# The gate of a Mamba block taken from VectorE: a copy on ScalarE and a product on GpSimd in its place

## What is computed

```
xi = silu(conv(xi) + conv_b)                 # 96 channels, L = 1024 steps
dbl = xi @ xp_w.T ;  dt, Bm, Cm = split(dbl)
delta = softplus(dt @ dt_w.T + dt_b)
dA = exp(delta * A) ; dBu = delta * Bm * xi
h  = dA_t * h + dBu_t                        # scan over L, 16 states a channel
y  = sum_s(h * C) + xi * Dp
y  = y * silu(z)                             # the gate
out = y @ out_w.T
```

## Time and profile before

| | |
|---|---|
| median of 3 runs | 4874.72 us |
| lowest and highest | 4870.76 and 4888.22 us |
| the profiled execution | 4889.31 us, of it 4886.7 us span on the core |
| granted TensorE clock, mean | 0.892 of full speed |
| busy PE, DVE, ACT, POOL | 85%, 74%, 57%, 48% |

### The profile page before, as it was taken

One profiled execution on the slowest core, in us unless ns is written; L12 is line 12 of the kernel. 1 busy time (PEld: TensorE's weight loads), 2 busy tenths in 40 slices (PEclk: granted clock), 3 DMA queues, 4 the chain that ended last, 5 costly groups with the idle time before them and its releaser, 6 DMA issues.

```text
span 4886.7 us, 48989 instructions
## 1 busy us (share of the span) xinstructions
PE 4157.1 (85%) x14248; PEld 1532.0 (31%) x14248; DVE 3639.2 (74%) x3157; ACT 2766.8 (57%) x3396; POOL 2334.7 (48%) x1084
## 2 busy tenths in 40 slices
PE   6779986899869998599986999769986799867997
PEld 2422233222332223322233222332233322332223
DVE  1469966699657996499864998559976599666996
ACT  2556645566455666466564664656646566465554
POOL 0137642467315773066630776227752376424663
PEclk9889998899878999799896998979998899987888
DMA  1147641567316772177622775237851476405661
GB/s 38 40 115 184 161 102 38 142 165 176 85 35 165 170 173 63 51 172 173 150 54 71 174 171 143 70 77 167 185 131 41 109 176 167 110 12 136 147 161 48
DMA packets 166840, 580.30 MB, mean 119 GB/s; under 512 B 22460, under 2 KB 23208, under 8 KB 162952
## 3 DMA queue, kind: packets, MB, share of 16 engines
q1 hardware_dynamic: 152168, 538.66, 46.0%
q10 hardware_dynamic: 14336, 37.76, 2.6%
HBM read 467.12 MB, written 71.48 MB: 110 GB/s over the span
## 4 chain that ended last, share of the span: by engine, by line
issue 30%; POOL 29%; PE 22%; ACT 9%; DVE 8%; DMA 1%; POOLq 0%; SPq 0%; DVEq 0%; ACTq 0%
POOL arena L1380 26%; PE ps L499 3%; PE ps L554 3%; PE ps L595 2%; PE ps L649 2%; DVE arena L1291 2%; ACT arena L819 2%; PE ps L545 2%; PE ps L714 2%; ACT arena L837 1%; POOL arena L1370 1%; PE ps L573 1%; PE ps L529 1%; POOL x L1388 1%; PE ps L695 1%
## 5 line engine op out<-in xcount | busy, mean ns | idle before, releaser
L1380 POOL TENSOR_TENSOR arena<-arena 128x1024 f32<-128x1024 f32 x768 | 1860.7, 2423 | 984.0 <-DVE arena L1291 984.0
L1291 DVE TENSOR_TENSOR_SCAN arena<-arena,ps 128x1024 f32<-128x1024 f32 x768 | 1756.3, 2287 | 96.1 <-ACT arena L994 1.0
L994 ACT ACTIVATE arena<-arena,a_all 128x1024 f32<-128x1024 f32 x768 | 867.2, 1141 | 427.0 <-DVE arena L1291 280.9
L1286 DVE TENSOR_TENSOR ps<-ps,arena 128x1024 f32<-128x1024 f32 x768 | 931.0, 1212 | 177.0 <-PE ps L697 176.2
L695 PE MATMUL ps<-arena,spread 32*128 32x512 f32 x1536 | 904.9, 677 | 130.6 <-DVE arena L1291 80.2
L697 PE MATMUL ps<-arena,spread 32*128 32x512 f32 x1536 | 891.5, 678 | 0.0
L714 PE MATMUL ps<-arena,gather 128*32 128x512 f32 x3072 | 550.1, 661 | 39.6 <-POOL arena L1380 39.6
L760 PE MATMUL ps<-x 96*96 96x512 f32 x1008 | 506.4, 621 | 0.0
L695 PEld LDWEIGHTS ps<-arena,spread 32*128 32x128 f32 x1536 | 235.7, 192 | 780.0 <-issue 386.8
L649 PE MATMUL ps<-arena,w_in 96*96 96x512 f32 x512 | 325.7, 795 | 65.6 <-DMA arena<-xq 64.8
L1334 POOL TENSOR_TENSOR x<-x,arena 96x512 f32<-96x512 f32 x64 | 109.4, 1709 | 431.9 <-DVE arena L1130 431.9
(11 more groups left out here) (158 smaller groups left out, 5672.2 us busy)
## 6 DMA issues: line engine op xcount, KB each, us to landing
arena<-dl SPq DMA_DIRECT2D x768, 512.0 KB, 5.8
dl<-arena ACTq DMA_DIRECT2D x64, 384.0 KB, 6.3
x<-pn SPq DMA_DIRECT2D x56, 247.5 KB, 6.0
arena<-in_x SPq DMA_DIRECT2D x9, 1536.0 KB, 10.6
arena<-xq SPq DMA_DIRECT2D x64, 192.0 KB, 7.9
arena<-arena ACTq DMA_DIRECT2D x64, 192.0 KB, 5.5
out<-x SPq DMA_DIRECT2D x64, 192.0 KB, 2.1
arena<-xq SPq DMA_DIRECT2D x64, 191.8 KB, 6.7
```

The costliest lines, as they stand in the source:

```text
L994: act.activation(da[:, m % DAS, :], dbc[:, m % DBC, :], ACT.Exp, scale=a_all[:, v // 2, m:m + 1]).then_inc(da_ready, 1)
L1286: dve.tensor_tensor(driven, driven, bmat[:, v % 2, :], ALU.mult).then_inc(bu_ready, 1)
L1291: dve.tensor_tensor_scan(hs[:, m % HSS, :], da[:, m % DAS, :], driven, 0.0, ALU.mult, ALU.add).then_inc(h_ready, 1)
L1380: pool.tensor_tensor(product, product, cmat[:, v % 2, :], ALU.mult).then_inc(pr_ready, 1)
```

## The change

The product y * silu(z) is split. ACT copies y from banks 0 and 1 to `yz` (`copy_y`, in slot `ACT_Y` = 2, ahead of that slot's decay; new semaphore `y_copied`), with the two waits that the gate had. POOL multiplies `yz` by `sz` in place (`gate`, in slot `POOL_GATE` = 1 behind that slot's product and ahead of `mix`), and `yz_ready` is now POOL's. PE's `skip` waits for `y_copied`. ACT's silu(z) leaves slot 1 and becomes the first work of slot 3 (`silu_z`, called by `early`), with a load of the silu table ahead and one of the exp and ln table behind it; the pair's first unit keeps it where it was. At the end of the pair the copy on ACT stands ahead of `mix_bias`, and the product on POOL ahead of `mix`.

```diff
-S_GATE, S_SKIP = 2, 3
+ACT_Y, POOL_GATE, S_SKIP, ACT_SILU_Z = 2, 1, 3, 3
...
                     if v:
-                        pe.wait_ge(yz_ready, p * UNITS + v)
+                        pe.wait_ge(y_copied, p * UNITS + v)
...
+                def silu_z(v):
+
+                    V = p * UNITS + v
+                    if v >= 2:
+                        act.wait_ge(yz_ready, V - 1)
+                    for c in range(2):
+                        act.wait_ge(z_ps, 2 * V + c + 1)
+                        act.activation(part(sz[:, v % 2, :], c), ps[0:DI, 6 + c, :],
+                                       ACT.Silu).then_inc(sz_ready, 1)
+
                 def early(slot, v):
...
+                    if slot == ACT_SILU_Z and v:
+                        act.preload_act_table(ACT.Silu)
+                        silu_z(v)
+                        exp_table()
...
-                        if v >= 2:
-                            act.wait_ge(yz_ready, V - 1)
-                        for c in range(2):
-                            act.wait_ge(z_ps, 2 * V + c + 1)
-                            act.activation(part(sz[:, i, :], c), ps[0:DI, 6 + c, :],
-                                           ACT.Silu).then_inc(sz_ready, 1)
+                        if v == 0:
+                            silu_z(v)
                         exp_table()
...
+                def copy_y(v):
+
+                    V = p * UNITS + v
+                    act.wait_ge(y_acc, (V + 1) * GPB)
+                    if v >= 2:
+                        act.wait_ge(mo_ready, 2 * (p * QUADS + v // 2))
+                    act.activation(yz[:, v % 2, :], two(0, DI), ACT.Copy).then_inc(y_copied, 1)
+
                 def step(v, m):
                     w, k = after(v, m, DAS - 1)
+                    if m == ACT_Y and v:
+                        copy_y(v - 1)
...
                 def final():
+                    copy_y(UNITS - 1)
                     if not last:
...
-                    dve.tensor_tensor(yz[:, v % 2, :], two(0, DI), sz[:, v % 2, :], ALU.mult).then_inc(yz_ready, 1)
...
+                    if m == POOL_GATE and v:
+                        gate(v - 1)
+
+                def gate(v):
+
+                    V = p * UNITS + v
+                    pool.wait_ge(y_copied, V + 1)
+                    pool.tensor_tensor(yz[:, v % 2, :], yz[:, v % 2, :], sz[:, v % 2, :],
+                                       ALU.mult).then_inc(yz_ready, 1)
...
-                scan_stage(prep, lambda: None, step, conv, lambda: None if last else mix(NCH - 1))
+                def final():
+                    gate(UNITS - 1)
+                    if not last:
+                        mix(NCH - 1)
```

More of the change, by code:

```diff
@@ L279, in program @@
         yz_ready = sem("yz_ready")
+        y_copied = sem("y_copied")
         mo_ready = sem("mo_ready")
@@ L1268, in prep @@
                         dve.tensor_tensor(delta, delta, soft, ALU.add).then_inc(delta_ready, 1)
-                def gate(v):
-                    V = p * UNITS + v
-                    dve.wait_ge(y_acc, (V + 1) * GPB)
-                    if v >= 2:
-                        dve.wait_ge(mo_ready, 2 * (p * QUADS + v // 2))
-                    dve.tensor_tensor(yz[:, v % 2, :], two(0, DI), sz[:, v % 2, :], ALU.mult).then_inc(yz_ready, 1)
                 def step(v, m):
@@ L1292, in step @@
                                            ALU.mult, ALU.add).then_inc(h_ready, 1)
-                    if m == S_GATE and v:
-                        gate(v - 1)
-                scan_stage(prep, lambda: None, step, lambda slot, v: None, lambda: gate(UNITS - 1))
+                scan_stage(prep, lambda: None, step, lambda slot, v: None, lambda: None)
                 for c in range(NG):
@@ L1392, in conv @@
                         mix(v - 1)
-                scan_stage(prep, lambda: None, step, conv, lambda: None if last else mix(NCH - 1))
+                def final():
+                    gate(UNITS - 1)
+                    if not last:
+                        mix(NCH - 1)
+                scan_stage(prep, lambda: None, step, conv, final)
                 if not last:
```

## The result

The changed kernel takes 4812.6 us in the median (four runs, 4802.47 to 4819.66), the kernel before, measured beside it, 4879.3 (four runs, 4870.76 to 4888.22): a ratio of 0.9862, with an interval of 0.9834 to 0.9889.

The account below looks back on a forecast made before the run. PE was taken to bound even units and DVE odd ones. Gains of 14, 6.5 and 5.6 us less 18.4 at the ends of the pairs made 7.7 us, for a median of 4867 us, range 4843 to 4894.

Follow-up runs that it names:

- the kernel with the decay put back: Changed kernel with ACT making the decay of slot 4 behind silu(z) in slot 3, not ahead of it: 4882.2 us, ratio 1.000 to the kernel before.

## What to carry to other kernels

When work is added to an engine's queue or moved in it, follow what its completion frees, a buffer and the transfer into it above all, until the end of the stage, not only what waits for it beside the change. Count an engine's idle time for every releaser before calling it full: a ceiling worked out from one of them is none. Where another engine sets the length of a stretch, that engine's work says what can be won there, and not the share of the waits that its name stands on. Where TensorE is nearly full, a wait of a microsecond or two late in a stage can cost several times its length, by the clock behind it, so it is worth having that edge in hand.

## What the hardware showed

A wait of 1.45 or 1.65 us on PE, in a stage where it is otherwise full, was followed by matmuls at 1.2 GHz and a unit 5.7 or 6.2 us longer than its 45.4; after one of 1.41 us at the end of another unit (pair 1 of the kernel with the decay put back) the next was only 1.1 longer, and in the kernel before, waits of 1.57 and 1.59 us (pairs 4 and 5) were followed by units of the usual 46.2. So no length of wait parts the two cases here. And the landing time of the same DMAs, with the same bytes, went with the place of one decay on ACT: the copy of u (192 KB) took 4.6 to 4.9 us in the median where the decay of slot 4 stands at 7.4 to 8.5 us, and 5.4 to 5.7 where it stands at 12.1 to 13.2.
